# A four-layer graph network on one core: turned probabilities and attention columns go through DRAM scratch instead of TensorE, and a low part moves to GpSimd

## The chip, the cores and the metric

One core of one Trainium2 chip runs the whole network on 64 graphs. The metric is the device time of one execution, in microseconds: lower is better.

## The reference

The input is x (64 graphs, 256 nodes, 256 features, fp32) and one adjacency matrix of 256 x 256. Four layers follow, each as x = layernorm(x + layer(x)):

```
L0: e = leaky(x W1 (x W2)^T); p = softmax(mask(e)); relu(p (x W3))
L1: h = x W; e = leaky(h a1 + (h a2)^T); p = softmax(mask(e)); elu(p h)
L2: o = relu(x mlp1 + b1); h = o W_fc; e = leaky(h a1 + (h a2)^T), unmasked
    o = elu(elu(softmax(e) h)) + o;   o3 = relu(o mlp2 + b2)
    masked graph attention on o3 with W_hand, a_hand; relu(elu(elu(..)) + o3)
L3: 4-head masked attention with wq, wk, wv, then wo
```

## The kernel before

Every matrix is held in fp32. A product of two matrices is made of three matmuls of reduced-precision pairs: each operand is split into a high part (a rounding copy, on ScalarE) and a low part (whole minus high, on VectorE or GpSimd), and `product3` issues (high, low), (low, high) and (high, high). With 256 nodes and 256 features a product is 12 matmuls of 128x256, or 24 where one side is 512 wide.

The work is a software pipeline over the graphs. Each engine has one order written out by hand in `ORDERS`: a list of steps with a stage number, as `t1:5`. In period k an engine runs through its whole list once, each step for graph k minus its stage. So there is no scheduling at run time: an instruction that waits holds up everything behind it on its engine. The period of the loop is the time from one graph to the next. SP's list holds the DMAs: two loads (`lt` x0T, `lx` x0), the store (`st`) and the round trip of the last layer's probabilities through DRAM scratch (`o40`, `i40`, `o42`, `i42`). In that trip VectorE turns 32x32 blocks (`turn4`, L950), one DMA writes them out, and four DMAs for 32 partitions each bring them back turned (L208).

What the change touches:

- The probabilities of layers 0, 1 and 2 (masked part) stand in `sco[i]`. TensorE turns them with four transposes each (`t0`, `t1`, `t3`, through `transposes`, L240) into PSUM; ScalarE copies the high part out, VectorE makes the low part (`low_part`, L692).
- `o3` turns `o3T` with four more transposes for the residual that VectorE adds in `r3` (L898).
- The attention columns h a2 come out of the product h (two extra columns, copied into `cols`). `spread` (L246) turns a column into a row on all partitions with a transpose of a broadcast column: `f1`, `f3` two each, `f2` four, and `b2` two for the reciprocal row sums of the unmasked attention. The sums themselves are eight matmuls with two columns (`d2`, L360).
- `z2` makes the low part of the mixed layer's second input `o2T` on VectorE; `n4` is the last normalization, on VectorE (L972); `k4` on GpSimd adds the output bias into `xb4`.

Order around the changed work, TensorE, per period before: 350 matmuls, ten stages (0 to 9).

Of the kernel before, what the change touches and what calls it, by code (L numbers as in the profile page):

```python
# [1113 lines left out]
```

## Time and profile before

| | |
|---|---|
| median of the runs shown (3 runs) | 2921.91 us (2917.68 to 2927.56) |
| the profiled execution | 2918.28 us |
| its span, first to last instruction | 2916.5 us |
| TensorE busy | 2689.4 us, 92% |
| VectorE busy | 2278.2 us, 78% |
| ScalarE busy | 1998.7 us, 69% |
| GpSimd busy | 1556.0 us, 53% |
| DMA queue of SP, share of 16 engines | 22.7%, 191.24 MB in 132464 packets |
| mean granted TensorE clock | 0.983 |

Busy is the time in which an engine has at least one instruction in work. TensorE's matmuls overlap in the records: a 128x256 matmul has a duration of 0.28 us but starts 0.12 us after the one before it, so costs on TensorE are read from the distances between starts. L12 is line 12 of the kernel. SPq is SP's instruction queue; PEld the weight load.

### The profile page before, as it was taken

To read this page: it belongs to the slowest core of one execution; us is meant where nothing else is said; L and a number is where in the kernel's file an instruction comes from. 1 tells how busy PE (TensorE), PEld (TensorE's weight loads), DVE (VectorE), ACT (ScalarE), POOL (GpSimd) and SP (SyncE) were. 2 spreads that over 40 slices of the span, in tenths; PEclk is the share of its full clock that TensorE was granted. 3 is DMA by queue.
4 is the path that set the end of the run, shared out by engine and by line. 5 is a ranking of instruction groups with operands and counts; after the bars stand their busy time and mean duration, and the time that the engine had idled before them with its cause. 6 is when DMAs were issued, how large, how long until landed. Compare 5 with 4: busy or idle time off the path is not lost.

```text
span 2916.5 us, 61536 instructions
## 1 busy us (share of the span) xinstructions
PE 2689.4 (92%) x22472; PEld 2551.3 (87%) x22472; DVE 2278.2 (78%) x6124; ACT 1998.7 (69%) x4801; POOL 1556.0 (53%) x2119
## 2 busy tenths in 40 slices
PE   4689999999999999999999999999999999999974
PEld 4589999999999999998999998999999999998863
DVE  3257888888888888888888887888888888888874
ACT  1357777777777776777777777777777777776752
POOL 0235555555555555555556555555655555555542
PEclk9799999999999999999999999999999999999997
DMA  3001222222122122212212221221222122122222
GB/s 109 19 16 37 77 81 64 57 81 80 41 80 81 59 63 80 74 47 81 80 51 71 81 72 49 81 81 48 74 81 70 52 80 80 41 81 73 66 66 73
DMA packets 132766, 195.17 MB, mean 67 GB/s; under 512 B 14832, under 2 KB 97136, under 8 KB 132464
## 3 DMA queue, kind: packets, MB, share of 16 engines
q1 hardware_dynamic: 132464, 191.24, 22.7%
q8 instruction: 178, 2.92, 0.4%
q14 instruction: 124, 1.02, 0.1%
HBM read 107.30 MB, written 83.89 MB: 66 GB/s over the span
## 4 chain that ended last, share of the span: by engine, by line
PE 60%; DMA 13%; ACT 8%; SPq 8%; DVE 6%; issue 4%; POOL 1%; POOLq 0%; DVEq 0%
PE ps L224 29%; DMA p4T<-scratch 10%; PE ps L378 6%; SPq L208 6%; PE ps L240 5%; PE ps L436 4%; PE ps L337 4%; PE ps L233 3%; PE ps L338 3%; DMA scratch<-p 3%; DVE p L950 3%; PE ps L456 2%; ACT p L671 2%; PE ps L360 2%; DVE h_lo L692 1%
## 5 line engine op out<-in xcount | busy, mean ns | idle before, releaser
L1067 POOL TENSOR_TENSOR p<-p,rd 128x512 f32<-128x512 f32 x256 | 269.8, 1054 | 20.0
L671 ACT ACTIVATE p<-p,nmx 128x256 f32<-128x256 f32 x512 | 255.7, 504 | 25.4 <-DVE nmx L935 25.2
L991 POOL TENSOR_TENSOR o1Tp_lo<-o1T,o1Tp_hi 128x1024 fp32r<-128x1024 f32 x64 | 153.8, 2403 | 220.8 <-ACT o1Tp_hi L472 220.8
L1003 POOL TENSOR_SCALAR xn<-act,nmean,rstd 128x256 f32<-128x256 f32 x384 | 243.6, 643 | 18.3 <-POOL rstd L998 11.2
L456 PE MATMUL ps<-p4T,v 128*64 128x256 f32 x1024 | 144.3, 404 | 118.2 <-DMA p4T<-scratch 117.7
L995 POOL TENSOR_TENSOR vare<-mv,eps 128x2 f32<-128x2 f32 x256 | 108.0, 422 | 270.5 <-DVE mv L748 270.5
L1060 POOL TENSOR_TENSOR rd<-some,den 128x2 f32<-128x2 f32 x256 | 53.5, 209 | 354.6 <-DVE den L944 354.6
L456 PEld LDWEIGHTS ps<-p4T,v 128*64 128x64 f32 x1024 | 67.3, 140 | 178.1 <-DMA p4T<-scratch 96.5
L692 DVE TENSOR_TENSOR xnT_lo<-ps,xnT_hi 128x512 fp32r<-128x512 f32 x192 | 132.1, 688 | 114.2 <-ACT xnT_hi L472 114.2
L935 DVE CUSTOM_DVE_ANT_0 p<-ps,mask 128x256 f32<-128x256 f32 x512 | 189.9, 418 | 33.3 <-PE ps L436 33.3
L480 ACT ACTIVATE sco<-sco,nmax 128x256 f32<-128x256 f32 x384 | 191.0, 500 | 28.9 <-DVE nmax L736 28.9
L991 POOL TENSOR_TENSOR x0Tp_lo<-x0T,x0Tp_hi 128x512 fp32r<-128x512 f32 x64 | 112.7, 1761 | 162.4 <-ACT x0Tp_hi L472 162.4
L472 ACT ACTIVATE h_hi<-ps 128x512 fp32r<-128x512 f32 x192 | 114.7, 597 | 112.9 <-PE ps L233 98.6
L998 POOL TENSOR_TENSOR rstd<-vare,mhalf 128x2 f32<-128x2 f32 x256 | 179.7, 702 | 0.0
L736 DVE CUSTOM_DVE_ANT_0 sco<-ps,mask 128x256 f32<-128x256 f32 x384 | 146.4, 417 | 40.0 <-ACT ps L475 40.0
L475 ACT ACTIVATE ps<-ps,cols 128x256 f32<-128x256 f32 x384 | 154.5, 441 | 33.7 <-PE ps L246 33.1
L612 ACT ACTIVATE o3T<-ps,b2m 128x256 f32<-128x256 f32 x128 | 53.8, 471 | 171.3 <-PE ps L378 171.3
L337 PE MATMUL ps<-w_fc_lo,o1Tp_hi 128*128 128x258 f32 x512 | 154.8, 302 | 8.5 <-POOL o1Tp_lo L991 5.9
L692 DVE TENSOR_TENSOR h_lo<-ps,h_hi 128x512 fp32r<-128x512 f32 x192 | 131.1, 683 | 38.4 <-ACT h_hi L472 38.4
L742 DVE BATCH_NORM_STATS2 stat<-act 128x6 f32<-128x256 f32 x384 | 143.4, 414 | 19.9 <-POOL act L1013 14.6
L950 DVE STREAM_TRANSPOSE p<-p 128x1024 f32<-128x1024 f32 x128 | 157.4, 1230 | 0.7 <-POOL p L1067 0.7
L224 PE MATMUL ps<-pfcp_lo,hfc_hi 128*128 128x256 f32 x512 | 155.6, 304 | 2.1 <-ACT rdb L472 2.1
(248 smaller groups left out, 12683.1 us busy)
## 6 DMA issues: line engine op xcount, KB each, us to landing
scratch<-p SPq DMA_DIRECT2D x128, 512.0 KB, 2.9
p4T<-scratch SPq DMA_DIRECT2D x512, 128.0 KB, 3.9
x0T<-in_xT SPq DMA_DIRECT2D x64, 256.0 KB, 4.6
x<-in_x SPq DMA_DIRECT2D x64, 256.0 KB, 3.7
out<-xn SPq DMA_DIRECT2D x64, 256.0 KB, 3.0
o1T<-in_mlp SPq DMA_DIRECT2D x1, 512.0 KB, 4.4
p<-in_mlp SPq DMA_DIRECT2D x1, 512.0 KB, 4.5
att<-in_fc SPq DMA_DIRECT2D x1, 512.0 KB, 5.4
```

The lines of the kernel that those rows point to most:

```text
L224: ins = nc.tensor.matmul(dst[:, m, :], lhs[a][:, k, (off + m) * P:(off + m + 1) * P], rhs[b][:, k, :], start=(k == 0 and i == 0), stop=(k ...
L337: nc.tensor.matmul(ps[:, 4, 0:C2], lhs, WP["fc"][b][:, k, 0:C2], start=(k == 0 and i == 0), stop=(k == HT - 1 and i == 2))
L456: ins = nc.tensor.matmul(bank[6][g * HD:(g + 1) * HD, c, :], v4[:, k, h * HD:(h + 1) * HD], p4Tv[:, c, g, k, :, :, :], start=(k == 0), sto ...
L480: ins = nc.scalar.activation(sco[i][:, m, :], sco[i][:, m, :], ACT.Exp, scale=-1.0, bias=nmax[i][:, m:m + 1], accum_out=den[i][:, m:m + 1])
L671: ins = nc.scalar.activation(rows_, rows_, ACT.Exp, scale=-1.0, bias=nmx4[:, h, m:m + 1], accum_out=den4[:, h, m:m + 1])
L692: return V.tensor_tensor(pair[1][:, :, :], whole, pair[0][:, :, :].bitcast(fp32), ALU.subtract)
L935: ins = V.tensor_tensor_reduce(p4v[h // 2][:, h % 2, m, :, :, :].rearrange("p w b j -> p w (b j)"), bank[7 - h % 2][:, m, :].rearrange("p ...
L950: V.transpose(p4[c][:, :, :], p4[c][:, :, :]).then_inc(S["p4x"], 1)
L991: return G.tensor_tensor(lo, whole, hi.bitcast(fp32), ALU.subtract)
L998: G.tensor_tensor(rstd[i][:, :], vare[i][:, :], mhalf[:, :], ALU.pow).then_inc(s_rs, 1)
L1003: ins = G.tensor_scalar(xn[:, m, :], y[:, m, :], nmean[i][:, m:m + 1], rstd[i][:, m:m + 1], ALU.add, ALU.mult)
L1067: G.tensor_tensor(rows_, rows_, rd4[:, h, :].unsqueeze(2).unsqueeze(3).broadcast_to([P, NT, QUADS, CT * QP]), ALU.mult).then_inc(S["p4n"], 1)
```

## The change

- `t0`, `t1`, `t3` move from TensorE to VectorE and SP. VectorE turns the 32x32 blocks of `sco[i]` into `act[i]` (`turn`), SP writes them to `scratch_pro[i]` (one DMA, `o0`, `o1`, `o3`) and reads them back into `sco[i]` (four DMAs, `i0`, `i1`, `i3`). ScalarE then copies the high part from SBUF, and GpSimd makes the low part (`low_of_turned`).
- `o3` goes the same way, through `sco[2]` and `scratch_o3` into the new tile `o3r` (`o5`, `i5` on SP); `r3` on VectorE becomes two instructions.
- The columns go through scratch too: `at_out` writes 256 single floats (`at2_out` 512) to DRAM, `at_in` reads them back with a broadcast to 128 partitions (`r1` and `f1`, `r3` and `f3`; `r2` and `f2`, the latter two DMAs). The leaky scores of layers 1 and 2 are then made in SBUF, not in PSUM.
- `d2` becomes four matmuls of 128x256 with a matrix of ones, which leaves the sums on all partitions; VectorE takes the reciprocal of 128x256 straight from PSUM, and `b2` is gone from TensorE and ScalarE.
- `z2` and `n4` move from VectorE to GpSimd; `xb4` is made in place in `xn2`; the output tile `xn3` is single.
- PSUM banks are given out anew (`enter` by bank), some tiles are shared or made in place, and all five orders are new, with nine stages on TensorE (0 to 8) and ten on GpSimd. Two orders shift against each other by a label where a list is cut at another place.

SP's list has 21 steps with 40 DMAs for a graph, where it had 7 steps with 13.

```
 ORDERS = {
-    "sp": "lt:0 o40:7 st:9 o42:7 lx:1 i40:7 i42:7",
-    "pe": "h3:8 a0:3 v4:9 f3:8 x0:5 g0:2 s40:9 d2:7 x1:6 t3:8 s42:9 v2:7 a3:8 m2:6 h0:2 b2:7 n2:6 o3:8 w2:7 s0:2 h1:5 c2:6 f1:5 t0:2 a4:9 r2:6 t1:5 x3:8 y4:9 m3:7 n3:7 a1:5 f2:6 q4:8 k4:8",
+    "sp": "o1:3 lt:0 f3:6 i1:3 i5:6 o3:6 o0:1 i3:6 i0:1 lx:1 o40:7 r1:2 i40:7 o42:7 f1:2 r2:4 i42:7 f2:4 o5:5 r3:5 st:8",
+    "pe": "g0:1 r2:5 a0:2 m3:6 h0:1 x1:4 a4:8 h3:6 m2:4 s0:1 x3:7 y4:8 d2:5 q4:7 k4:7 x0:2 v4:7 n2:4 s40:7 w2:5 v2:5 s42:7 a1:3 h1:2 c2:4 a3:6",
+    "ac": "w2:6 x2:6 s0:2 x3:8 m2:5 p0:2 q4:8 u3:7 l0:1 k4:8 p3:7 t1:4 n2:5 x0:3 p40:8 o2:5 p41:8 y2:6 p42:8 a1:4 t3:7 p43:8 k2:6 c2:5 h1:3 t0:2 a3:7 z2:6 b3:7 r2:5 g0:1 a0:2 u1:3 m3:6 o3:6 x1:4 p1:3 h0:1 f2:5 h3:6 a4:8",
+    "dv": "r3:7 r2:5 z3:7 g0:1 e1:3 st3:7 o3:6 st0:2 ag3:7 ag0:2 x1:4 f2:5 i1:3 t1:3 h0:1 b2:5 h3:6 a4:8 x3:7 e0:1 y4:8 st4:8 d2:5 q4:7 ag4:8 e3:6 i0:1 k4:7 v4:7 t3:6 t0:1 i3:6 s40:7 s41:7 x0:2 p40:7 v2:5 s42:7 p41:7 s43:7 i2:5 p42:7 n2:5 b1:3 a1:3 x40:7 p43:7 j2:5 c2:4 h1:2 c3:6 x42:7 b3:6 st1:3 a3:6 ag1:3",
+    "po": "w2:6 n0:3 v4:9 l0:1 t1:4 d40:8 p40:8 m2:5 d41:8 p41:8 d42:8 t3:7 y1:4 d43:8 p42:8 p43:8 t0:2 z2:6 v1:4 k4:8 n1:4 a0:2 m3:6 v3:7 v0:2 n4:9 n3:7",
 }
...
+            def turn(i):
+                blocks = sco[i][:, :, :, :].rearrange("p b a n -> p (b a) n").rearrange("p c (w j) -> p w c j", w=QUADS)
+                return V.transpose(flat(act[i]).rearrange("p (w c j) -> p w c j", w=QUADS, j=QP), blocks)
...
+            def pro_out(i):
+                def step(t):
+                    sp.wait_ge(S[f"pro{i}_x"], t + 1)
+                    wait(sp, S[f"pro{i}_dma"], back(t - 1))
+                    sp.dma_start(scratch_pro[i].rearrange("p w n -> p (w n)"), flat(act[i])).then_inc(S[f"pro{i}_dma"], 16)
+                return step
+            def pro_in(i):
+                def step(t):
+                    sp.wait_ge(S[f"pro{i}_dma"], sent(t))
+                    rows_ = sco[i][:, :, :, :].rearrange("p b a n -> p (b a n)").rearrange("p (q n) -> p q n", q=QUADS)
+                    for w in range(QUADS):
+                        sp.dma_start(rows_[w * QP:(w + 1) * QP, :, :], scratch_pro[i][:, w, :].rearrange("(q j) n -> j q n", q=QUADS)).then_inc(S[f"pro{i}_dma"], 16)
+                return step
...
+            def at2_out(t):
+                sp.wait_ge(S["at2"], t + 1)
+                wait(sp, S["at2_dma"], back(t - 1, 2))
+                sp.dma_start(scratch_at[2].rearrange("m p -> p m"), cols[2][:, :, :].rearrange("p m c -> p (m c)"), allow_slow_non_contiguous=True).then_inc(S["at2_dma"], 16)
+            def at2_in(t):
+                sp.wait_ge(S["at2_dma"], sent(t, 2))
+                wait(sp, S["u"], t)
+                for c in range(2):
+                    sp.dma_start(by_tiles(row2[:, c, :]), scratch_at[2][c::2, :].unsqueeze(0).broadcast_to([P, NT, P])).then_inc(S["at2_dma"], 16)
...
+            def low_of_turned(pair, i):
+                source = sco[i][:, :, :, :].rearrange("p b a n -> p (b a n)").rearrange("p (q c i) -> p c q i", q=QUADS, i=QP)
+                lo, hi = (flat(h).rearrange("p (c q i) -> p c q i", q=QUADS, i=QP) for h in (pair[1], pair[0]))
+                return low_part(lo, source, hi)
```

## Rows read from the trace of the kernel before

**Rows 1.** The page's own busy line of TensorE and its weight loads, VectorE, ScalarE, GpSimd.

```profile
PE 2689.4 (92%) x22472; PEld 2551.3 (87%) x22472; DVE 2278.2 (78%) x6124; ACT 1998.7 (69%) x4801; POOL 1556.0 (53%) x2119
```

**Rows 2.** Busy by stretch, 29 periods: stretch, length, engines, PEclk, DMA share, GB/s.

```profile
376.66:1613.71 1237.05, 1192.14 (x10152) 1137.90 (x10151) 1018.61 (x2756) 903.53 (x2176) 707.93 (x957) 1.00 0.24 69
```

**Rows 3.** SP's queue, timeline: stores of the first and thirty-first graph (start, us).

```profile
333.75 0.43 SPq L194 DMA_DIRECT2D out<-xn  x1
...
1613.71 0.43 SPq L194 DMA_DIRECT2D out<-xn  x1
```

**Rows 4.** TensorE, timeline of one period: start us, us of the group, line.

```profile
1572.53 0.60 PE L240 MATMUL ps<-ident,o3T 128*128 128x128 f32 x4
1572.88 0.37 PE L224 MATMUL ps<-pfcp_lo,hfc_hi 128*128 128x256 f32 x1
1573.09 0.28 PE L224 MATMUL ps<-pfcp_hi,hfc_lo 128*128 128x256 f32 x1
1573.20 0.28 PE L224 MATMUL ps<-pfcp_hi,hfc_hi 128*128 128x256 f32 x1
...
1580.17 0.38 PE L246 MATMUL ps<-ident,cols 128*128 128x128 f32 x2
1580.39 0.60 PE L240 MATMUL ps<-ident,sco 128*128 128x128 f32 x4
...
1604.14 0.27 PE L360 MATMUL ps<-ones,pfcp_lo 128*128 128x2 f32 x1
...
1605.06 0.65 PE L240 MATMUL ps<-ident,xn 128*128 128x128 f32 x4
```

**Rows 5.** Waits of TensorE on the scratch trip: us in total, times, longest.

```profile
PE ps L456 <- DMA p4T<-scratch: 117.7, 92, 12.4
```

**Rows 6.** DMA issues on the page: count, KB each, median us from issue to landing.

```profile
scratch<-p SPq DMA_DIRECT2D x128, 512.0 KB, 2.9
p4T<-scratch SPq DMA_DIRECT2D x512, 128.0 KB, 3.9
...
x<-in_x SPq DMA_DIRECT2D x64, 256.0 KB, 3.7
```

**Rows 7.** SP's queue, timeline of one period's DMAs.

```profile
1574.43 0.52 SPq L190 DMA_DIRECT2D x<-in_x  x1
1575.05 4.02 SPq L208 DMA_DIRECT2D p4T<-scratch  x8
1579.11 0.43 SPq L186 DMA_DIRECT2D x0T<-in_xT  x1
```

**Rows 8.** Stretches of 1 us in a burst: TensorE busy, PEclk, DMA share, GB/s.

```profile
1532.00:1533.00 1.00, 1.00 (x11) 1.00 1.14 401
...
1538.00:1539.00 1.00, 0.00 (x0) 1.00 1.09 242
```

**Rows 9.** VectorE groups, whole span: busy us, mean ns, idle before.

```profile
L950 DVE STREAM_TRANSPOSE p<-p 128x1024 f32<-128x1024 f32 x128 | 157.4, 1230 | 0.7 <-POOL p L1067 0.7
L736 DVE CUSTOM_DVE_ANT_0 sco<-ps,mask 128x256 f32<-128x256 f32 x384 | 146.4, 417 | 40.0 <-ACT ps L475 40.0
L860 DVE TENSOR_TENSOR att<-ex,att 128x1024 f32<-128x1024 f32 x64 | 92.5, 1446 | 0.2
L692 DVE TENSOR_TENSOR o2T_lo<-att,o2T_hi 128x1024 fp32r<-128x1024 f32 x64 | 79.7, 1246 | 66.6 <-ACT o2T_hi L472 66.6
L972 DVE TENSOR_SCALAR xn<-xn,nmean,rstd 128x256 f32<-128x256 f32 x128 | 66.9, 562 | 1.1 <-POOL rstd L998 1.1
L898 DVE TENSOR_TENSOR act<-act,ps 128x512 f32<-128x512 f32 x64 | 44.0, 688 | 7.0 <-DVE act L801 0.5
```

**Rows 10.** ScalarE groups, whole span.

```profile
L480 ACT ACTIVATE sco<-sco,nmax 128x256 f32<-128x256 f32 x384 | 191.0, 500 | 28.9 <-DVE nmax L736 28.9
L472 ACT ACTIVATE h_hi<-ps 128x512 fp32r<-128x512 f32 x192 | 114.7, 597 | 112.9 <-PE ps L233 98.6
L475 ACT ACTIVATE ps<-ps,cols 128x256 f32<-128x256 f32 x384 | 154.5, 441 | 33.7 <-PE ps L246 33.1
```

**Rows 11.** GpSimd groups, whole span.

```profile
L991 POOL TENSOR_TENSOR o1Tp_lo<-o1T,o1Tp_hi 128x1024 fp32r<-128x1024 f32 x64 | 153.8, 2403 | 220.8 <-ACT o1Tp_hi L472 220.8
L991 POOL TENSOR_TENSOR o3Tp_lo<-o3T,o3Tp_hi 128x512 fp32r<-128x512 f32 x64 | 82.3, 1286 | 107.7 <-ACT o3Tp_hi L472 107.7
```

More of the change, by code:

```diff
@@ L132, in graph_stack @@
         rd4 = sb("rd4", [P, HEADS, NT])
-        xb4 = sb("xb4", [P, NT, C])
-        xn3 = [sb(f"xn3_{i}", [P, NT, C]) for i in range(2)]
+        xn3 = sb("xn3", [P, NT, C])
         STAGED = ("W1T", "W2T", "W_T", "hand_T")
@@ L169, in graph_stack @@
         scratch = [nc.dram_tensor(f"scratch{c}", [P, QUADS, 2 * NT * CT * P // QUADS], fp32, kind="Internal").ap() for c in range(2)]
+        scratch_pro = [nc.dram_tensor(f"scratch_pro{i}", [P, QUADS, NT * N // QUADS], fp32, kind="Internal").ap() for i in range(3)]
+        scratch_o3 = nc.dram_tensor("scratch_o3", [P, QUADS, CT * N // QUADS], fp32, kind="Internal").ap()
+        scratch_at = {i: nc.dram_tensor(f"scratch_at{i}", [c * NT, P], fp32, kind="Internal").ap() for i, c in ((1, 1), (2, 2), (3, 1))}
         n_loads = len(weights) - 2 + 2 + HT + 2
@@ new lines, in o3_in, with at_out, step @@
+            def o3_in(t):
+                sp.wait_ge(S["o3_dma"], sent(t))
+                wait(sp, S["r3"], t)
+                rows_ = o3r[:, :, :, :, :].rearrange("p q k a c -> p q (k a c)")
+                for w in range(QUADS):
+                    sp.dma_start(rows_[w * QP:(w + 1) * QP, :, :], scratch_o3[:, w, :].rearrange("(q j) n -> j q n", q=QUADS)).then_inc(S["o3_dma"], 16)
+            def at_out(i):
+                def step(t):
+                    sp.wait_ge(S[f"at{i}"], t + 1)
+                    wait(sp, S[f"at{i}_dma"], back(t - 1, 1))
+                    sp.dma_start(scratch_at[i].rearrange("m p -> p m"), cols[i][:, :, 1], allow_slow_non_contiguous=True).then_inc(S[f"at{i}_dma"], 16)
+                return step
@@ L240, in transposes @@
                         ins = nc.tensor.transpose(dst[:, b, a * P:(a + 1) * P], src[:, a, b * P:(b + 1) * P], ident[:, :])
-                return ins
-            def spread(dst, col):
-                for m in range(NT):
-                    ins = nc.tensor.transpose(dst[:, m * P:(m + 1) * P], col(m).broadcast_to([P, P]), ident[:, :])
                 return ins
@@ L355, in d2 @@
             def d2(t):
                 pe.wait_ge(S["pfcl"], t + 1)
-                for m in range(NT):
-                    for k in range(NT):
-                        for i in (1, 0):
-                            ins = nc.tensor.matmul(ps[:, 5, 2 * m:2 * m + 2], pfcp[i][:, k, m * P:(m + 1) * P], ones2[:, :],
-                                                   start=(k == 0 and i == 1), stop=(k == NT - 1 and i == 0))
+                enter(5, "rdb", t + 1)
+                for k in range(NT):
+                    for i in (1, 0):
+                        ins = nc.tensor.matmul(ps[:, 5, 0:N], ones2[:, :], pfcp[i][:, k, :], start=(k == 0 and i == 1), stop=(k == NT - 1 and i == 0))
@@ L375, in mlp2 @@
-            def mlp2(m):
-                for k in range(HT):
-                    for i, (a, b) in enumerate(PAIRS):
-                        ins = nc.tensor.matmul(bank[3][:, m, :], WP["mlp2"][a][:, k, m * P:(m + 1) * P], o2T[b][:, k, :],
-                                               start=(k == 0 and i == 0), stop=(k == HT - 1 and i == 2))
-                return ins
+                pe.wait_ge(S["pfcl"], t + 1)
+                enter(5, "att", t + 1)
+                product3(half_of(5), hfc, pfcp, NT, 2, off=2).then_inc(S["w2_mm"], 1)
@@ L395, in f3 @@
[L395 to L401 removed]
+                enter(2, "h3", t + 1)
+                enter(3, "h3", t + 1)
+                product3(lambda m: ps[:, 2 + m, 0:C2], o3Tp, WP["hand"], CT, NT).then_inc(S["h3_mm"], 1)
             def a3(t):
@@ L895, in r3 @@
             def r3(t):
-                dv.wait_ge(S["on3_mm"], t + 1)
+                dv.wait_ge(S["o3_dma"], back(t))
                 dv.wait_ge(S["q3"], t + 1)
-                V.tensor_tensor(act[2][:, :, :], act[2][:, :, :], bank[2], ALU.add).then_inc(S["r3"], 1)
+                for m in range(NT):
+                    row = act[2][:, m, :].rearrange("p (k q c) -> p k q c", k=CT, q=QUADS)
+                    ins = V.tensor_tensor(row, row, o3r[:, :, :, m, :].rearrange("p q k c -> p k q c"), ALU.add)
+                ins.then_inc(S["r3"], 1)
             def z3(t):
```

414 lines of the change are left out of this document (234 added, 180 removed), and 3 rows, old and new, of the table ORDERS.

## The prediction

> **What bounds the kernel now.** I read the page's busy line first: TensorE is at work for 92% of the span [rows 1]. In the middle of the run its share is 1192.1 of 1237.1 us, 96%, with full clock [rows 2]. The loop is steady: thirty graphs lie between two stores at 333.75 and 1613.71 us, so a period is 42.67 us [rows 3]. The timeline of one period then says what fills it. A 128x256 matmul starts 0.119 us after the one before (the matmuls from 1573.09 on, [rows 4]), so a product of twelve takes 1.43 us. The one long wait of TensorE inside a period is for the scratch trip of the last layer: 117.7 us in all, 1.84 us a graph [rows 5]. So TensorE's own work of about 40.6 us (below) plus this wait gives the period. The other engines, over the same stretch and per period of 42.67 us: VectorE 35.1, ScalarE 31.2, GpSimd 24.4 us [rows 2]. The DMA engines are busy 0.24, 10.2 us a period.
>
> **TensorE's part.** Removed: sixteen transposes in four groups. A group of four spans 0.35 us (1572.53 to 1572.88) and makes the matmul behind it 0.09 us late (0.21 instead of 0.12 to the next), so 0.44 each [rows 4], 1.76 in all. Ten spread transposes at 0.11 (1580.17 to 1580.39 for two), 1.1 us. `d2` falls from 0.92 (1604.14 to 1605.06, eight) to 4 x 0.119 = 0.48. Together 3.3 us a graph. What is left: 16 products of 1.43, three of 24 matmuls at 2.87, three groups of transposes at 0.44, `d2` 0.48, the fp32 product `a4` about 2.1 and the two score steps about 0.95 each (estimates from the same timeline): 37.3 us. TensorE alone would allow a period of 37.3 us.
>
> **What the others get.** Per period:
> - VectorE loses three low parts of 128x512 (0.69 each, the length of the 128x512 row from PSUM), `z2` 1.25, `n4` 2 x 0.56 and a small reciprocal 0.15: 4.6 us. It gets four block transposes of 128x512 at half of 1.23, 2.5 us [rows 9]; `r3` in two pieces, +0.15 (two at 0.42 against 0.69); and a reciprocal of 128x256. The trace has none of this size; the nearest of 256 elements is the masked step's 0.42 [rows 9], which is the low end, and I keep four times it, 1.7, as the high end. I take 0.45, as every 256-element row of VectorE lies near it. Net -1.5: 33.6 us.
> - GpSimd gets three low parts of 128x512 at 1.29, `z2` at 2.40 [rows 11] and `n4` at about 1.3: 7.6 us, so 32.0.
> - ScalarE loses the copy of `rdb`, 0.4: 30.8.
> - SP goes from 13 to 40 DMAs. One issue takes 0.43 to 0.52 us (eight in 4.02, [rows 7]): 17 to 21 us. The out-DMA must have landed before its in-DMA is issued, and SP waits in order.
> - DMA engines: packets in a burst move 401 GB/s with 4 KB packets and 242 GB/s with 1 KB packets, all engines busy [rows 8], which is 163 and 68 ns a packet; a straight line gives 52 ns at 512 B and 36 ns at 4 B (estimate). Per graph the change adds 512 packets of 2 KB, some 3070 of 512 B and 1024 of 4 B, about 250 us on 16 engines, 15.5 us. 10.2 + 15.5 is 0.64 of a 40 us period. The engines hold, but bursts will meet.
>
> No engine's sum passes 37.3. But with five queues at 77 to 93% and fixed orders, the chains between them decide. I followed two.
>
> **Chain one, attention columns of the unmasked layer.** From `r2` on TensorE to `d2` in the same period TensorE has a0, m3, h0, x1, a4, h3, m2, s0, x3, y4: 14.4 us. In that time go: high part 0.60, column copy 0.15, out 2.9, issue 0.5 and in 3.7 [rows 6], maximum 0.43, three leaky 1.28, subtraction 0.68, exp 0.62, high 0.63, low on GpSimd 1.29, with about 0.9 of hand-offs, and `h3` and `a4` of ScalarE ahead of the exp, 0.5 beyond what is parallel: 14.2. Nothing is spare. Before, this path had spreads of 0.45 us and a stage more.
>
> **Chain two, probabilities of the second graph attention.** After `h3` on TensorE: high 0.60 [rows 10], columns 0.16, out 2.9, in 3.7, two leaky 0.88, two masked 0.85 [rows 9], two exps 1.38 with their read-outs [rows 10], block transposes 0.62, out 2.9, four issues up to the last 1.55 and its landing 3.9, high 0.62, low 1.29, hand-offs 1.2: 22.5 us; `k4` and `v4` of VectorE stand ahead of `t3`, +0.7. It must end before `a3`, the last step of TensorE's list; lows and landings are those of [rows 6, 11]. From there to the next `h3` TensorE has 14.0 us of work, with `h3` and the seven steps ahead of it, and `a3` 1.43. One turn: 23.2 + 14.0 + 1.4 = 38.6 us. This, not TensorE's 37.3, is the floor.
>
> Two more hand-offs are as tight: `i42` is issued behind `r2`, so the second half of `a4` gets its data at 11.2 to 12.0 us in TensorE's period against 11.5 needed; and GpSimd goes from `m3` through `v3`, `v0`, `n4` to `n3` (6.2 us without a pause) with about 0.5 us before `x3` on TensorE. Before, the period stood 2.1 us over TensorE's sum, 1.84 of it one DMA wait. I take 1.6 us over the floor for the new set of such waits: a period of 40.2 us.
>
> **Sum.** 42.67 - 40.2 = 2.47 us, times 63 periods, 156 us. Filling the pipeline has one stage less on TensorE, but the first periods are bound by one graph's chain, which gets up to 7 us for each trip: I set these against each other at nothing, -30 to +40. 2918.28 - 156 = 2762 us. The profiled execution stands 3.6 us below the median, within the spread of the runs.
>
> **The skill's rules.** On VectorE the two-input operation that reads SBUF twice takes 1446 ns (L860) where the row of the same size and kind L692 has 1246 [rows 9], so some hold-up is in the rows. The Trainium skill, page SBUF — State Buffer, section Who interferes with whom, says that a VectorE instruction with two SBUF inputs contends with a GpSimd instruction that reads SBUF; by it `e1`, `e3` and `b2`, whose input leaves PSUM, become exposed. The trace agrees in L860. It gives the third case below.
>
> **Rivals.**
> - *TensorE stays the bound.* If landings are shorter than 2.9 and 3.7 us for these smaller transfers (64 to 128 KB), both chains fall below TensorE's sum, and the period is about 38.4: 2918 - 63 x 4.3 = 2648. For it: the in-trip of 3.9 us is read in a burst of eight. Against: more bursts than before. 0.13.
> - *The forecast*, 39.2 to 41.2 a period, 2700 to 2826. 0.52.
> - *VectorE and GpSimd hold each other up.* 3.2 us of VectorE's work becomes two-input from SBUF and GpSimd is 80% busy; at up to a half more, and with some DMA queueing, the period is 41.3 to 42.5: 2830 to 2908. 0.11.
> - *The column trips cost more than they save.* Place: `at2_out` and `at_out`, single floats to DRAM, on the path of both chains. Price: if a 4-byte write takes two 1 KB packets' time, 136 ns, then 512 of them take 4.4 us instead of 1.2; chain one has no slack, so the period is floor + 1.6 + 3.2 and more with `i42` queued behind it on the same rings: about 43.8, 2918 + 63 x 1.1 = 2990. It decides for slower once a column trip is 2.5 us over my 7.1. The rows have no 4-byte transfer on the path, so nothing speaks against it but the straight line. 0.21.
> - Exactly within the measurement: 0.03. (About 0.3% is what a measurement of this kernel can tell from no change.) That the change doesn't do what it says, I leave in these: matmuls would still count 350 a graph.
>
> The Trainium skill, page DMA: Bandwidth & Descriptors, section Rules for kernel authors, says a strided last dimension becomes one descriptor per element, and its Specifications that under 512 B the engine does read-modify-write. That rule would make the last rival true; no run here shows its price yet.
>
> **Chances.** Faster 0.13 + 0.52 + 0.11 = 0.76, same 0.03, slower 0.21. The range reaches from within the first rival to the slow one: 2660 to 2985.
>
> **What would show it.** In the profile after: 350 - 16 - 10 - 4 = 320 matmuls a graph; a period between stores near 40.2; TensorE 93% busy with waits named at `a3`, `d2` and `a4`, on GpSimd's `proT_lo`, `pfcp_lo` and DMA; GpSimd near 32 us a period; DMA share near 0.6. I am wrong if TensorE's waits lie at steps of VectorE with no trip behind them, if a column's out-DMA lands later than 4 us, if the reciprocal takes over 1 us, or if TensorE's clock falls in the waits.

## The result, and the profile after

Median of the changed kernel: 4600.14 us (4 runs, 4596.38 to 4612.86), against 2923.6 us before (4 runs, 2917.68 to 2927.56). The ratio is 1.5745, 95% interval 1.5703 to 1.5787. I had forecast 2762 us, with a range up to 2985. The profiled execution took 4598.71 us, with a span of 4596.9 us.

The page's busy rows and the granted clock by fortieths of the span, after:

```profile
PE 2889.1 (63%) x20552; PEld 2618.2 (57%) x20552; DVE 2342.2 (51%) x6060; ACT 1993.7 (43%) x4737; POOL 2105.1 (46%) x2503
PEclk8778788788778787787787788778788778778776
```

Against [rows 1]: TensorE has fewer matmuls (20552 over 64 graphs are 321 each, the set-up among them; I had said 320), so the change does what it says. But no engine is at work for even two thirds of the span, and the granted clock is 0.7 to 0.8 where it had been full [rows 2]. Every engine waits. The chain that ended last, by engine and by line, says for whom:

```profile
DMA 52%; PE 23%; DVE 15%; issue 4%; SPq 4%; ACT 1%; POOL 1%; DVEq 0%; POOLq 0%; ACTq 0%
DMA scratch<-p 22%; PE ps L303 17%; DMA out<-xn 16%; DMA p4T<-scratch 10%; PE ps L499 3%; SPq L286 3%; DVE p L1047 2%; DMA scratch_at<-cols 2%; DVE p L1032 2%; DVE att L943 2%; DVE att L948 2%; DVE act L889 1%; PE ps L473 1%; PE ps L313 1%; DVE xn L1058 1%
```

Over half of it is DMA, and the transfers named (`scratch<-p`, `out<-xn`, `p4T<-scratch`) are ones that the kernel before had too. The list of issues (KB each, median us from issue to landing) shows how they have changed against [rows 6]:

```profile
scratch<-p SPq DMA_DIRECT2D x128, 512.0 KB, 17.1
p4T<-scratch SPq DMA_DIRECT2D x512, 128.0 KB, 7.0
scratch_pro<-act SPq DMA_DIRECT2D x192, 256.0 KB, 2.1
sco<-scratch_pro SPq DMA_DIRECT2D x768, 64.0 KB, 2.0
scratch_at<-cols SPq DMA_DIRECT2D x64, 2.0 KB, 13.4
```

`scratch<-p` lands after 17.1 us instead of 2.9, `p4T` after 7.0 instead of 3.9. Both medians are of the second half of the probabilities (`o42`, `i42`) alone: for the first half the trace names no landing, and in the period below SP reads it back 2.8 us after it was written (2046.38 to 2049.14). The new trips of the probabilities are fast (2.1 out, 2.0 back, where I had put 2.9 and 3.7). The slow one is `scratch_at<-cols`: 2 KB in 13.4 us. One period of SP's queue (start, length, line, transfer, count):

```profile
2013.26 0.36 SPq L252 DMA_DIRECT2D scratch_at<-cols  x1
2013.67 0.46 SPq L216 DMA_DIRECT2D out<-xn  x1
...
2015.27 0.34 SPq L208 DMA_DIRECT2D x0Tp<-in_xT  x1
2023.76 0.37 SPq L260 DMA_DIRECT2D sco<-scratch_at  x1
...
2048.68 0.37 SPq L252 DMA_DIRECT2D scratch_at<-cols  x1
2049.14 1.84 SPq L286 DMA_DIRECT2D p4T<-scratch  x4
2051.43 0.34 SPq L278 DMA_DIRECT2D scratch<-p  x1
2058.93 0.38 SPq L260 DMA_DIRECT2D sco<-scratch_at  x1
2059.40 0.92 SPq L266 DMA_DIRECT2D scratch_at<-cols  x1
2069.82 1.75 SPq L286 DMA_DIRECT2D p4T<-scratch  x4
...
2081.98 0.46 SPq L216 DMA_DIRECT2D out<-xn  x1
```

The store comes at 2013.67 and again at 2081.98: this period is 68.3 us, and over 35 graphs of the steady part the mean is 68.9, against 42.67 [rows 3]. In it SP stands still three times while a column write is out: 2015.61 to 2023.76, 2051.77 to 2058.93, 2060.32 to 2069.82, together 24.8 us. The first two waits are for the write itself: from `r3` to the read `f3` that waits for it are 10.5 us, from `r1` to `f1` 10.25. The third is for the second half of `p`, issued at 2051.43 behind `r1` and read back at 2069.82, 18.4 us later. (A fourth long stand, 2073.37 to 2081.57, is for VectorE's `cols`.) Stretches of that period, with the busy time of TensorE, its weight loads, VectorE, ScalarE, GpSimd, then the granted clock and the DMA share:

```profile
2060.00:2070.00 10.00, 0.00 (x0) 0.00 (x0) 0.00 (x0) 0.00 (x0) 0.00 (x0) 0.67 0.39 92
2000.00:2010.00 10.00, 3.34 (x16) 1.38 (x13) 2.28 (x7) 2.38 (x8) 4.11 (x10) 0.50 0.50 104
2047.20:2048.20 1.00, 1.00 (x11) 1.00 (x10) 1.00 (x3) 0.83 (x3) 1.00 (x2) 1.00 1.00 414
2049.00:2050.00 1.00, 1.00 (x10) 1.00 (x9) 1.00 (x2) 0.16 (x1) 1.00 (x2) 1.00 0.15 1
2052.00:2057.00 5.00, 4.30 (x36) 4.09 (x36) 4.44 (x12) 1.82 (x4) 5.00 (x6) 1.00 0.22 9
```

From 2060 to 2070 no compute engine does anything. The last three rows show what the DMA engines do around the write of `r1` (issued at 2048.68). At 2047.20 the first half of `p` goes out at 414 GB/s. The packets of the column write itself are few and short: 272 of them in the microsecond from 2049, at a DMA share of 0.15. By 2052 four reads of 128 KB and the 512 KB of the second half have been issued behind it. Until 2057 all queues together move 9 GB/s, at a share of 0.22. So the column write doesn't fill the DMA engines. While it is unfinished, the transfers behind it crawl.

Near the waits TensorE is granted 0.50, the lower of its two levels (1.2 GHz). TensorE's busy time in the steady part is 827.90 of 1300 us, at a period of 68.9 us 43.9 us a graph, more than before (41.1, by [rows 2]) for 30 matmuls fewer.

### The profile page after: what moved, and what is told of

Same layout as the page of the kernel before. It is cut to its first block, busy times and chain, and to the rows that moved or that the text cites. A ratio compares the mean times of both kernels' runs of the same rounds, so it can differ in the third digit from the quotient of the medians.

```text
span 4596.9 us, 63285 instructions
## 1 busy us (share of the span) xinstructions
PE 2889.1 (63%) x20552; PEld 2618.2 (57%) x20552; DVE 2342.2 (51%) x6060; ACT 1993.7 (43%) x4737; POOL 2105.1 (46%) x2503
## 4 chain that ended last, share of the span: by engine, by line
DMA 52%; PE 23%; DVE 15%; issue 4%; SPq 4%; ACT 1%; POOL 1%; DVEq 0%; POOLq 0%; ACTq 0%
DMA scratch<-p 22%; PE ps L303 17%; DMA out<-xn 16%; DMA p4T<-scratch 10%; PE ps L499 3%; SPq L286 3%; DVE p L1047 2%; DMA scratch_at<-cols 2%; DVE p L1032 2%; DVE att L943 2%; DVE att L948 2%; DVE act L889 1%; PE ps L473 1%; PE ps L313 1%; DVE xn L1058 1%
## 5 line engine op out<-in xcount | busy, mean ns | idle before, releaser
L517 ACT ACTIVATE sco<-sco,cols 128x256 f32<-128x256 f32 x256 | 116.1, 500 | 1407.8 <-DMA sco<-scratch_at 1407.8
L313 PE MATMUL ps<-ident,xn 128*128 128x128 f32 x768 | 169.9, 364 | 755.1 <-ACT o3T L677 751.3
L313 PEld LDWEIGHTS ps<-ident,xn 128*128 128x128 f32 x768 | 123.4, 188 | 767.9 <-issue 765.5
L808 DVE CUSTOM_DVE_ANT_0 sco<-sco,mask 128x256 f32<-128x256 f32 x256 | 96.9, 416 | 877.0 <-ACT sco L517 876.9
L499 PE MATMUL ps<-p4T,v 128*64 128x256 f32 x1024 | 247.2, 635 | 258.5 <-DMA p4T<-scratch 258.5
L303 PE MATMUL ps<-xnT_lo,w_wkT_hi 128*128 128x256 f32 x256 | 113.0, 441 | 447.2 <-DVE xn L1058 447.2
L1082 POOL TENSOR_TENSOR pfcp_lo<-pfcp,pfcp_hi 128x512 fp32r<-128x512 f32 x64 | 82.3, 1286 | 496.8 <-ACT pfcp_hi L514 496.8
L1154 POOL TENSOR_TENSOR rd<-some,den 128x2 f32<-128x2 f32 x256 | 180.3, 704 | 214.9 <-DVE den L1041 214.8
L303 PE MATMUL ps<-h_lo,proT_hi 128*128 128x256 f32 x512 | 160.3, 313 | 50.1 <-POOL proT_lo L1082 50.1
L303 PE MATMUL ps<-o2T_lo,w_mlp_hi 128*128 128x256 f32 x512 | 152.9, 299 | 55.4 <-POOL o2T_lo L1082 41.9
## 6 DMA issues: line engine op xcount, KB each, us to landing
scratch<-p SPq DMA_DIRECT2D x128, 512.0 KB, 17.1
```

What stands on the lines that cost most here:

```text
L303: ins = nc.tensor.matmul(dst(m), lhs[a][:, k, (off + m) * P:(off + m + 1) * P], rhs[b][:, k, :], start=(k == 0 and i == 0), stop=(k == kt ...
L313: ins = nc.tensor.transpose(dst[:, b, a * P:(a + 1) * P], src[:, a, b * P:(b + 1) * P], ident[:, :])
L499: ins = nc.tensor.matmul(bank[6][g * HD:(g + 1) * HD, c, :], v4[:, k, h * HD:(h + 1) * HD], p4Tv[:, c, g, k, :, :, :], start=(k == 0), sto ...
L1082: return G.tensor_tensor(lo, whole, hi.bitcast(fp32), ALU.subtract)
L1154: G.tensor_tensor(rd4[:, h, :], some3[:, :], den4[:, h, :], ALU.mult).then_inc(S["rd4"], 1)
```

## The experiments

Ratios are against the kernel before on the same chip. A period is the mean distance of stores over 35 graphs of the steady part.

**The write by itself.** A kernel of DMAs alone; it leaves out the whole network and copies the first input to the output. SP issues one DMA, waits until it has landed, then issues the next, six times each form.

```
one = (d256.rearrange("m p -> p m"), cols[:, :, 1])                          # as r1, r3
two = (d512.rearrange("m p -> p m"), cols[:, :, :].rearrange("p m c -> p (m c)"))  # as r2
(d8, cols[:, :, 1])             # 256 floats end to end, in another order
(d8w[:, 0:NT], cols[:, 0, :])   # 128 pieces of 8 B, 512 B apart
(d4w[:, :, 0], cols[:, :, 1])   # 256 floats, 64 B apart
(d128, turned[1::QP, :])        # four runs of 128 B
go(one, (dbig, big))            # the write, 512 KB behind it
```

> This kernel leaves the whole network out. SP issues one DMA at a time and waits until it has landed, six times each: 256 single floats to DRAM with a transposed order (the r1 and r3 write of the change), 512 of them (the r2 write), 128 pairs of 8 bytes next to each other, 128 pairs 512 bytes apart, 256 floats 64 bytes apart, four runs of 128 bytes, the broadcast read of f1, 256 single floats read back, 512 KB in rows of 4 KB, and last the first write with the 512 KB behind it in the queue. Theory one (a single float written to DRAM is slow by itself): the first write takes 8 to 10 us against about 2 us for the four runs and the 512 KB write's 2.9 us, the second takes longer still, and the 512 KB write behind the first one lands at 11 us or later. Theory two (the writes are slow in the changed kernel only because 40 DMAs a graph queue on the same rings): each of them takes 2 to 3.5 us here. If the cause is that neighbouring floats share a block of DRAM, the floats 64 bytes or 512 bytes apart are fast; if it is the count of pieces, they are as slow.

SP's queue (start, length of the row, transfer, count):

```profile
2.31 101.89 SPq L50 DMA_DIRECT2D floats<-cols  x12
113.09 35.78 SPq L50 DMA_DIRECT2D pairs_dense<-cols  x6
156.04 7.37 SPq L50 DMA_DIRECT2D pairs_apart<-cols  x6
164.50 10.62 SPq L50 DMA_DIRECT2D floats_apart<-cols  x6
176.48 8.25 SPq L50 DMA_DIRECT2D runs<-turned  x6
185.79 15.22 SPq L50 DMA_DIRECT2D wide_in<-floats  x6
203.59 10.54 SPq L50 DMA_DIRECT2D back<-floats  x6
215.82 13.45 SPq L50 DMA_DIRECT2D rows4k<-big  x6
231.56 0.37 SPq L50 DMA_DIRECT2D floats<-cols  x1
231.97 0.47 SPq L50 DMA_DIRECT2D rows4k<-big  x1
242.64 0.37 SPq L50 DMA_DIRECT2D floats<-cols  x1
```

From one row's start to the next's, over the count, is the time of one DMA with its landing. The first row holds six writes of 256 floats (8.9 us each, the seventh starts at 55.93) and six of 512 (9.5 us). `pairs_dense` takes 7.2 us. It was meant as 128 pairs of 8 B, but its source is the column of single floats, and the trace has 272 packets for one of these writes, as for one of 256 floats, against 144 for one of `pairs_apart`. So it is 256 floats end to end in another order. From the same column, 256 floats 64 B apart take 2.0 us. 128 real pairs 512 B apart take 1.4; four runs of 128 B 1.6; the broadcast read 3.0; the 256 floats read back 2.0; 512 KB in rows of 4 KB 2.6.

Twice the pieces cost 0.6 us more, which is inside the scatter of single writes (8.4 to 9.6 and 8.2 to 10.6). The same number of packets from the same column, 64 B apart, costs under a third. So what costs is that many pieces go to neighbouring addresses, not how many or how small they are. The DMA engines' busy share over the first 50 us, in slices of 1.25 us, shows where the time goes:

```profile
DMA  0010000001000000100000010000001000000010
```

The packets of a write are at work in one slice of the seven. The others hold no packet at all, and only at their end is the landing told. The last three rows of the table: the write with 512 KB issued behind it takes 11.1 us (231.56 to 242.64), near the sum of the two alone (8.9 + 2.6), not the longer of them. A transfer behind the write is held up by it.

**The columns back on TensorE.** All of the change stays but the column trips; `f1`, `f2`, `f3` are the spread transposes of the kernel before, and SP has 33 DMAs a graph.

```diff
-    sp: "... f3:6 ... r1:2 ... f1:2 r2:4 ... f2:4 ... r3:5"
-                sp.dma_start(scratch_at[i].rearrange("m p -> p m"), cols[i][:, :, 1], ...)
-                sp.dma_start(tile[:, :, 0, :], scratch_at[i].unsqueeze(0).broadcast_to([P, NT, P]))
+            def f1(t):
+                pe.wait_ge(S["at1"], t + 1)
+                spread(ps[:, 1, 0:N], lambda m: cols[1][:, m, 1:2]).then_inc(S["f1_mm"], 1)
-                graph_scores(sco[1], 1).then_inc(S["raw1"], 1)
+                graph_scores(sco[1], by_tiles(ps[:, 1, 0:N]), 1).then_inc(S["raw1"], 1)
```

> The changed kernel with its three column trips undone: eight transposes of broadcast columns on TensorE make the rows in PSUM again, and SP has 33 DMAs a graph instead of 40. All else stays. Theory one (the column writes are the cause, and they also hold up every DMA behind them): the period falls from 68.9 us to 39 to 42 us, 2650 to 2850 us in all, with TensorE at full clock. Theory two (40 DMAs a graph, the four-fold scratch trips and SP's fixed order bound the loop): the period stays above 55 us, over 3600 us in all.

Measured: 2830.29 us, ratio 0.9712 (0.9692 to 0.9733), period 41.1 us. So the column trips alone make 27.8 us a graph (68.9 - 41.1), all of the loss and more. `p4T<-scratch` lands in 3.0 us, sooner than before the change (3.9). The steady part, in the columns given above:

```profile
700.00:2000.00 1300.00, 1244.27 (x10390) 1168.15 (x10388) 1156.84 (x2980) 976.50 (x2352) 1072.04 (x1236) 1.00 0.39 123
```

Full clock. Per period of 41.1 us: TensorE 39.3, VectorE 36.5, ScalarE 30.8, GpSimd 33.9.

**The columns through DRAM, written fast.** VectorE turns the columns in a 32x32 block first, so that each write has four runs of 128 B. All reads stay.

```diff
-                    sp.dma_start(scratch_at[i].rearrange("m p -> p m"), cols[i][:, :, 1], ...)
+                    for m in range(NT):
+                        sp.dma_start(scratch_at[i][m, :].rearrange("(w j) -> w j", w=QUADS), turned[i][2 * m + 1::QP, :])
+                V.transpose(turned[i][:, :], wide[i][:, :]).then_inc(S[f"at{i}"], 1)
```

> The changed kernel with the same three trips through DRAM at the same places, but VectorE first turns the columns in a 32x32 block, so that each write DMA moves four runs of 128 bytes; two writes instead of one for r1 and r3, four for r2, so 45 DMAs a graph. Theory one (the single-float pieces are the cause): a write lands within 2 to 3 us, the period is 39 to 43 us, 2650 to 2900 us. Theory two (round trips through DRAM and their number are the cause, whatever their pieces): no better than 4600 us, since five DMAs a graph are added.

Measured: 2955.28 us, ratio 1.0133 (1.0106 to 1.016), period 42.9 us, 55 us above the range that I had given. The clock is full again (1.00 in the steady part), so 26.0 of the 27.8 us were the write's form. But even so this kernel loses to the spreads of TensorE by 1.8 us a period. Of this I can't split off the turning, which gives VectorE 1.2 us a graph more to do (copies and block transposes), nor the five more DMAs. The waits (waiter and what it waits for: us in all, times, longest):

```profile
ACT sco L521 <- DMA sco<-scratch_at: 162.5, 100, 4.3
DVE fmax L933 <- DMA row<-scratch_at: 72.8, 50, 4.2
```

ScalarE waits 2.5 us a graph for the rows of `f1` and `f3`. VectorE waits 1.1 us a graph for that of `f2`, the trip on chain one.

**One such write in the kernel before.** Nothing else is changed. A 256-float write of `mhalf`, which nothing reads, stands ahead of `i40`.

```diff
-    "sp": "lt:0 o40:7 st:9 o42:7 lx:1 i40:7 i42:7",
+    "sp": "lt:0 o40:7 st:9 o42:7 lx:1 c1:7 i40:7 i42:7",
+                sp.dma_start(scratch_small.rearrange("m p -> p m"), mhalf[:, :], allow_slow_non_contiguous=True).then_inc(S["small"], 16)
```

> The kernel before with one DMA added for each graph: 256 single floats written to DRAM from a constant tile, issued just ahead of the reads that bring the last layer's probabilities back; nothing waits for its data but the next such write. Theory one, with its second half (the DMAs behind a small write wait for it on the rings): the reads land about 8 us later, TensorE waits for them, the period rises from 42.7 by 6 to 9 us, 3300 to 3500 us in all. Rival (only the steps that need the column suffer): no more than one issue, 0.4 us a graph, 2925 to 2955 us.

Measured: 3513.18 us, ratio 1.2051 (1.2022 to 1.208), period 52.0 us: the theory's mechanism, a little over its range. Its DMA issues, its wait that answers to [rows 5], and its steady part:

```profile
p4T<-scratch SPq DMA_DIRECT2D x512, 128.0 KB, 10.6
scratch_small<-mhalf SPq DMA_DIRECT2D x64, 1.0 KB, 9.8
PE ps L463 <- DMA p4T<-scratch: 562.4, 106, 19.6
700.00:2000.00 1300.00, 1089.32 (x8753) 1014.83 (x8752) 878.73 (x2375) 778.32 (x1876) 608.53 (x827) 0.90 0.23 57
```

A write whose data nobody needs adds 9.3 us a graph. `p4T` lands 6.7 us later than in [rows 6]. TensorE's wait for it grows from 117.7 to 562.4 us, by 6.9 us a graph. TensorE's busy time grows from 41.1 to 43.5 us a graph at a clock of 0.90. 6.9 and 2.4 are the 9.3. So the harm is in what is held behind the write and in the clock that is lost in the wait.

**The writes on another queue.** The change whole, with the three column writes issued by ScalarE, in an order of its own, so that they are not ahead of SP's transfers in SP's queue.

```diff
-    sp: "... r1:2 ... r2:4 ... r3:5 ..."
+    ac: "... t0:2 r1w:3 a3:7 ... g0:1 r2w:5 a0:2 ... a4:8 r3w:6"
-                    sp.dma_start(scratch_at[i].rearrange("m p -> p m"), cols[i][:, :, 1], ...)
+                    nc.scalar.dma_start(scratch_at[i].rearrange("m p -> p m"), cols[i][:, :, 1], ...)
```

> The changed kernel with its three column writes issued by ScalarE instead of SP, otherwise the same trips with the same single floats. Two parts of the loss are told apart. If the 9 us of a write are paid by its own trip and, on SP's queue, by every DMA behind it, then here only the trip pays: the period is the second chain's 38.6 with 9 instead of 2.9 us, and the waits, 46 to 50 us, 3150 to 3450 us in all, and the last layer's probabilities land in 3 to 4 us again. Rival (a slow write holds the 16 DMA engines themselves, whatever queue it came from): the other transfers still land after 8 us and more, 4300 to 4650 us.

Measured: 4264.46 us, ratio 1.4599 (1.455 to 1.4648), period 63.5 us. My theory, by which SP's queue was the most of it, missed by over 800 us; the rival's range begins 36 us above the measurement. The issue line of `scratch<-p`, a part of one period of SP's rows with ScalarE's first write in it, and a stretch in the columns of the result above:

```profile
scratch<-p SPq DMA_DIRECT2D x128, 512.0 KB, 12.8
2013.47 0.34 SPq L265 DMA_DIRECT2D scratch<-p  x1
2015.64 0.37 ACTq L744 DMA_DIRECT2D scratch_at<-cols  x1
2016.55 1.74 SPq L273 DMA_DIRECT2D p4T<-scratch  x4
2019.64 0.34 SPq L265 DMA_DIRECT2D scratch<-p  x1
2032.44 1.74 SPq L273 DMA_DIRECT2D p4T<-scratch  x4
2019.00:2023.00 4.00, 1.68 (x14) 1.51 (x13) 4.00 (x10) 1.29 (x3) 2.05 (x3) 1.00 0.35 12
```

The first half of `p`, out before the column write is issued, is read back after 3.1 us. The second half, issued 4.0 us behind a column write that is on another engine's queue, takes 12.8 us (the median of all second halves too), and in the stretch 2019 to 2023 all queues together move 12 GB/s, as they did in the changed kernel. So the slow write holds up transfers of other queues as well. With e1 and e4 this is the same mechanism at three places. Taking the writes out of SP's queue gave back 5.4 of the 27.8 us, in this one order, in which ScalarE waits for them in SP's stead. What in the chip makes neighbouring writes slow, no run shows.

**What sets the 41.1 us.** With the columns on TensorE the kernel is near my forecast of 40.2 us, 0.9 us a period above it. VectorE is 2.9 us above my sum. I took the term that was most off, the reciprocal of 128x256, away first: the sum of `pfcp` is read as a column, turned over on 128x2, spread by TensorE, copied by ScalarE.

```diff
-                V.reciprocal(rdb[:, :], ps[:, 5, 0:N]).then_inc(S["rdb"], 1)
+                V.reciprocal(rdc[:, :], ps[:, 5, 0:4:2]).then_inc(S["rdc"], 1)
+            def b2(t):
+                spread(ps[:, 5, N:2 * N], lambda m: rdc[:, m:m + 1]).then_inc(S["b2_mm"], 1)
```

> The changed kernel with its columns back on TensorE (as in e2_columns_on_pe, 41.1 us a period), and in addition the row sums of the unmasked attention as in the kernel before: eight matmuls with two columns, a reciprocal of 128x2, two spread transposes and a copy on ScalarE, in place of a reciprocal of 128x256, which takes 1.74 us. TensorE gets about 0.8 us of work more, VectorE 1.6 us less. Theory one (with the column trips gone, VectorE's in-order list, 89% busy, sets the period, and the mis-sized reciprocal is a term of it): the period falls by 0.8 to 1.5 us, 2735 to 2780 us. Rival (TensorE or GpSimd sets it): unchanged or up to 0.8 us slower, 2825 to 2880 us.

Measured: 2832.99 us, ratio 0.9697 (0.9672 to 0.9723), period 41.0: no change against the run with the columns back. VectorE's busy share in the steady part falls to 1111 of 1300 us, 35.1 a period, and the period doesn't follow. The edit also adds to TensorE (39.9 us busy instead of 39.3), so it shows that VectorE's sum alone is not the bound, and not what the reciprocal by itself is worth. TensorE is busy for 96% of the steady part, as it was before the change [rows 2]; that its list with a few short waits is the bound is a rival that no run tests.

Then work from GpSimd back to VectorE: `n4`, on top of the edit just shown; and, in another kernel, `z2` alone.

```diff
-    po: "... v0:2 n4:9 n3:7"
+    dv: "... x40:7 n4:8 ..."
+                    ins = V.tensor_scalar(xn3[:, m, :], xn3[:, m, :], nmean[3][:, m:m + 1], rstd[3][:, m:m + 1], ALU.add, ALU.mult)
```

> e5_small_reciprocal with the last normalization back on VectorE (1.1 us there, 1.58 us on GpSimd). Theory one (VectorE alone sets the period): slower than e5_small_reciprocal by 0.5 to 1.1 us a period, 30 to 70 us. Rival (the two engines' lists end each other's waits, and GpSimd's share counts as much): faster by up to 0.8 us a period, 10 to 50 us, the best version so far.

```diff
-                low_part(o2T[1][:, :, :], att[:, :, :], o2T[0][:, :, :]).then_inc(S["o2T"], 1)   # gpsimd
+                low_part(o2T, att[:, :, :]).then_inc(S["o2T"], 1)                                # vector
```

> e2_columns_on_pe (2830 us) with one part of the change undone: the low part of the mixed layer's second input is made on VectorE again (1.25 us) and not on GpSimd (2.58 us). Theory one (VectorE's list sets the period): slower, 2860 to 2920 us. Rival (GpSimd's list sets it; in the chain that ended last it has more steps than any other): faster, 2740 to 2810 us.

Measured: 2866.74 us, ratio 0.9812 (0.9782 to 0.9843), and 2862.86 us, 0.9804 (0.9778 to 0.983); both periods 41.6. Each is 0.5 to 0.6 us a graph worse than leaving the work on GpSimd. So for these two pieces the change's own idea, low part and norm on GpSimd, is right. Both lie where the theory of VectorE's list had put them, and the small reciprocal where its rival had: work added to VectorE costs, work taken from it brought nothing.

GpSimd is the odd one in the trace of the kernel with the columns back. From 1499.80 to 1530.1 us it has no pause, and in it are rows like these (start, length, line, operation):

```profile
1499.80 0.20 POOL L1151 TENSOR_TENSOR rd<-some,den 128x2 f32<-128x2 f32 x1 [2.39 <-DVE den L1038]
...
1503.45 1.17 POOL L1151 TENSOR_TENSOR rd<-some,den 128x2 f32<-128x2 f32 x1
...
1540.87 0.20 POOL L1151 TENSOR_TENSOR rd<-some,den 128x2 f32<-128x2 f32 x1 [2.37 <-DVE den L1038]
```

The same two numbers to a partition take 0.20 us once and 1.17 us another time; the mean is 0.71, where the kernel before had 0.21. I moved this product to VectorE: first with the small reciprocal, then with the wide one kept, then with operations of one column and one input from the tile.

```diff
-                    G.tensor_tensor(rd4[:, h, :], some3[:, :], den4[:, h, :], ALU.mult).then_inc(S["rd4"], 1)
+                    V.tensor_tensor(rd4[:, h, :], some3[:, :], den4[:, h, :], ALU.mult).then_inc(S["rd4"], 1)
```

> e5_small_reciprocal (2833 us, 41.0 us a period) with the four tiny products rd = some3 x den a graph made on VectorE, each behind its reciprocal, and no longer on GpSimd, where one takes 0.71 us on the average and stands in the chain that ended last. GpSimd loses about 3 us a graph, VectorE gets 0.7 us. Theory (a loop through GpSimd's list and TensorE's scores sets the period, not the sum of any engine): the period falls by 1.5 to 2.8 us, 2660 to 2740 us. Rival (VectorE's list sets it): up to 0.7 us slower, 2835 to 2880 us.

> e2_columns_on_pe with the same edit, so that the reciprocal of 128x256 (1.74 us on VectorE) stands in, and TensorE has 0.8 us less than in e9_rd_on_vector. If, with GpSimd relieved, VectorE's list is what ends last, this is slower than e9_rd_on_vector by 0.5 to 1.6 us a period (30 to 100 us); if TensorE is, it is faster by up to 0.8 us (50 us).

```diff
+                    for m in range(NT):
+                        ins = V.tensor_scalar(rd4[:, h, m:m + 1], den4[:, h, m:m + 1], some3[:, m:m + 1], None, ALU.mult)
```

> e9_rd_on_vector (2891 us) with each tiny product rd = some3 x den made by two one-column operations that take some3 as a scalar operand, so that only one tensor input comes from SBUF. There the two-input product of 128x2 took 0.54 us on the average and 1.07 us where GpSimd's 128x512 product was at work. Theory (VectorE's second SBUF input waits for GpSimd's read to end): a one-column operation takes 0.06 to 0.2 us whatever GpSimd does, and the period falls by 0.8 us or more, to 2780 to 2840 us, at or below e5_small_reciprocal. Rival (VectorE's place in the order costs it, not the input): 2880 us or slower.

Measured: 2891.28 us, ratio 0.9907 (0.989 to 0.9924); 2892.35 us, 0.9915 (0.9891 to 0.9939); 2985.8 us, 1.0216 (1.0178 to 1.0254). The rows of the first and of the third (count: shortest/median/longest ns, stretch):

```profile
L1052 DVE TENSOR_TENSOR rd<-some,den x256: 160/172/1072, 234.3 to 2867.7; 128x2 f32<-128x2 f32 x128
L1053 DVE TENSOR_SCALAR rd<-den,some x512: 202/210/216, 231.2 to 2960.0; 128x1 f32<-128x1 f32 x171
```

All three are slower than the versions that they start from, where my theories had said faster. On VectorE too the two-input product takes up to 1.07 us, and 0.16 where nothing is in its way. With one column it is never long. But the time grows with it, so the long product was not what costs. That the place in VectorE's order costs is what is left of my two readings; it isn't shown. With the wide reciprocal kept (2892.35) nothing changes against the small one (2891.28). Why the third is 94 us above the first, with shorter operations but 256 more of them, stays open. I didn't find an order for VectorE that pays.

**The best version again**, on another chip, with no edit.

> The same kernel as e2_columns_on_pe, beside e11_rd_one_input on the same chip: 2820 to 2840 us again, about 0.97 of the kernel before.

Measured: 2832.79 us, ratio 0.9694 (0.9663 to 0.9725). It beats both kernels: about 3% below before.

## Why the prediction was wrong

*The step that failed* is the term "out 2.9" for an attention column, in both chains. I took it from the landing of the 512 KB write in [rows 6], as if a landing went with the transfer. Alone a column's write takes 8.9 us, in the kernel 10.3 to 10.5. Beside it I priced the 4-byte packets by a straight line through those of 4 KB and 1 KB, 36 ns each, and concluded that the engines hold. The line had nothing at its far end, since no row of before has a small piece on the path. But it erred to the dear side: 272 packets at a share of 0.15 of 16 engines for 1 us are 9 ns each. The time of such a write doesn't go by its packets. It lies between the last of them and the landing, and it goes by the distance of the pieces in DRAM: 256 floats side by side 7.2 to 8.9 us, 64 B apart 2.0.

*The fourth rival named the place* and the threshold (slower once a trip is 2.5 us over my 7.1), and I gave it 0.21. Its mechanism was not the one that the runs show, since it too priced packets, at 136 ns. It came to 43.8 us a period, where 68.9 was measured, so its being on the right side is in part luck. Two terms were missing in it and in my sum:
- The write holds up every transfer behind it, of any queue. I had this only as "`i42` queued behind it".
- While all wait, TensorE's clock falls. I had named this as a sign and put it at nothing. With the same matmuls, TensorE is busy for 39.0 us a graph at full clock when the columns are written fast (e3), and for 43.9 at 0.80 in the changed kernel: 4.9 of the 26.0 us between the two.

Of the four signs by which I would be wrong three came true: the write lands after more than 4 us, the reciprocal takes over 1 us, and the clock falls in the waits.

*The rule of the skill that spoke against the change.* The Trainium skill, page DMA: Bandwidth & Descriptors, says in Rules for kernel authors that a strided last dimension becomes a descriptor per element, and in Specifications that under 512 B the engine does read-modify-write. The trace agrees with the first: 272 packets for a write of 256 floats in e1. It agrees with the second in the direction: 9.8 us for the 1 KB write in e4. But the page's 512 B isn't what separates fast from slow here: pieces of 4 B that lie 64 B apart take 2.0 us, pieces of 8 B that lie 512 B apart 1.4 us.

*What the kernel with the columns back says of the other steps:*
- TensorE loses work: right in kind. It has 328 matmuls a graph, and its busy time falls by 1.8 us (41.1 to 39.3); by my terms for what is left out there (16 transposes 1.76, two spreads 0.22, `d2` 0.44) it would be 2.4. With the matmuls of the change (e3) it is busy for 39.0 us, where I had 37.3.
- ScalarE 30.8: as said. GpSimd 33.9 where I had 32.0: the products of `rd` are 4 x (0.71 - 0.21) = 2.0 us more.
- VectorE 36.5 where I had 33.6. The reciprocal takes 1.74 us, at the high end that I had kept and not taken; four block transposes 0.69 each, not 0.62. These are 1.6 of the 2.9 us. Another 0.5 is `r3`, whose two pieces take 0.68 us each, not 0.42 (first row: mean ns of one behind the busy time). Some 0.5 more is in the masked steps with both inputs in SBUF, with a mean of 538 ns (second row; the last two rows have shortest/median/longest ns, with one input in PSUM in the last):

```profile
L990 DVE TENSOR_TENSOR act<-act,o3r 128x256 f32<-128x256 f32 x128 | 81.4, 675 | 0.3
L805 DVE CUSTOM_DVE_ANT_0 sco<-sco,mask 128x256 f32<-128x256 f32 x256 | 128.8, 538 | 3.2 <-ACT sco L511 3.1
L805 DVE CUSTOM_DVE_ANT_0 sco<-sco,mask x256: 387/416/1515, 91.2 to 2758.3; 128x256 f32<-128x256 f32 x128
L805 DVE CUSTOM_DVE_ANT_0 sco<-ps,mask x128: 414/419/426, 55.4 to 2556.9; 128x256 f32<-128x256 f32 x128
```

  With both inputs in SBUF most of these steps take the same 416 ns as with one in PSUM, and some take up to 1.5 us. In the changed kernel, where GpSimd is at work for 46% of the span and not 76%, the longest of them takes 427 ns. The Trainium skill, page SBUF — State Buffer, section Who interferes with whom, says that a VectorE instruction with two SBUF inputs contends with a GpSimd instruction that reads SBUF; the trace agrees, with 0.12 us on the average here. The third rival was right that this exists. (The prediction's own pair of rows was no test of it: L860 and L692 both read SBUF twice, and take 1446 and 1246 ns.) e5 shows that VectorE's sum doesn't set the period; what GpSimd loses in the same way, 2.0 us a graph in `rd`, was only tried together with a change of orders (e9, e10).
- DMA engines: 0.39 of 41.1 us are 16.0 us without the column trips, and 0.42 of 42.9 are 18.0 with them written fast; my sum for all of the change was 25.7. The packets were cheaper than my line, down to those of 4 B.
- Chain two: GpSimd's unbroken 30 us, then TensorE's scores and VectorE's masked steps, back to GpSimd's `rd` at 1540.87, is a loop of a period. I had taken the loop through `a3` with a floor of 38.6 and 1.6 of waits: 40.2. It is 41.1. But that floor had a column's trip of 6.6 us in it, which this kernel doesn't make; without it my chain is 32.0 us long and can't be what sets 41.1. So it is luck that the two numbers are close. Nor did the first rival come: its condition, shorter landings, holds here (2.4 us out, 2.0 back), but its period of 38.4 us did not come. That GpSimd's loop sets it is read off the trace; the moves off GpSimd, e6, e7, e9 and e10, didn't shorten it, so it isn't shown.
- Filling and draining: I set it at nothing. 63 periods of 1.60 us would give 101 us, and the gain over the kernel before is 83 us. Some 18 us are lost at the ends.
- Chain one: I had it with nothing spare. In e3, with a fast write, VectorE still waits 1.1 us a graph for this chain's row, which fits; that the chain has no slack at all isn't shown.

## What to carry to other kernels

A trip through DRAM that turns a column needs its price measured as a form, before it is summed. Here a write whose pieces of 4 bytes lie side by side in DRAM cost 9 us and held back all other transfers, and turning the column on chip first, for runs of 128 B, took the same write to 1.6 us. Don't take the landing of a large write, or a line through large packets, as the price of a small write of another form: look for the time between its last packet and its landing. Where the spread of a rival's price is unknown, ask what else is on the same DMA engines, since that multiplies it. Where a chain across engines sets the time, removing a long operation from a busy engine (the reciprocal, 1.7 us a graph) may bring nothing, and moving small ones to another's queue may cost more than they take.

## What the runs showed of the hardware

- A DMA write to DRAM of 256 floats to neighbouring addresses takes 8.9 us (7.2 in another order), of 512 floats 9.5; with the floats 64 B apart 2.0, pairs 512 B apart 1.4. Its packets are at work for no more than 1.25 us of that. Reading the same 256 floats takes 2.0 us.
- It holds back others, of its own queue and of another engine's: with 512 KB behind it both are done after 11.1 us, where the 512 KB alone take 2.6; with the slow writes on ScalarE's queue, the second half of `p` on SP's lands after 12.8 us, and the first half, out before such a write, is read back after 3.1 in the period shown. Meanwhile all DMA engines together move 9 to 12 GB/s, against 414 just before.
- A reciprocal of 128x256 takes 1.74 us on VectorE, four times the masked step of that size.
- A product of 128x2 with two inputs in SBUF takes 0.16 us on VectorE or 0.20 on GpSimd when free, and up to 1.07 and 1.17 us beside work of the other engine; an operation on one column, with one such input, stays at 0.20 to 0.22 on VectorE.
- A masked step of 128x256 with both inputs in SBUF takes 0.42 us, and up to 1.5 us in the kernel that keeps GpSimd at work for 76% of the span; with one input in PSUM it never takes more than 0.43.
